# Reordering the first loads and splitting the last output products of a four-layer cross-attention and expert kernel on Trainium2

## The reference

```python
x = x + L0_xattn(layernorm(x), ctx, ...)      # 16 heads of 16, 1601 context rows of 192, with biases
x = x + L0_ffn(layernorm(x), ...)             # 16 experts, top 4 by groups, and a shared expert
x = x + L1_xattn(...);  x = x + L1_ffn(...)   # 16 heads; 8 experts, top 2, gelu
x = x + L2_xattn(...);  x = x + L2_ffn(...)   # 8 heads of 32; 8 linear experts, top 2
x = x + L3_xattn(..., mask, ...); x = x + L3_ffn(...)   # 16 heads, masked keys; 16 gated experts, top 2

# one attention
q, k, v = xn @ Wq + bq, ctx @ Wk + bk, ctx @ Wv + bv      # split by heads
att = softmax(q @ k.T * scale)                            # over the 1601 context rows
out = (att @ v) @ Wo + bo                                 # heads joined again
```

## Time and profile before

| | |
|---|---|
| median of 3 runs | 3855.93 us (3853.42 to 3857.38) |
| the profiled execution | 3857.22 us, its span 3855.5 us |
| mean granted TensorE clock in it | 0.966 of full |
| PE, DVE, ACT, POOL busy | 94%, 66%, 50%, 17% of the span |

### The profile page before, as it was taken

One profiled execution on the slowest core, in us unless ns is written; L12 is line 12 of the kernel. 1 busy time (PEld: TensorE's weight loads), 2 busy tenths in 40 slices (PEclk: granted clock), 3 DMA queues, 4 the chain that ended last, 5 costly groups with the idle time before them and its releaser, 6 DMA issues. The chain is left out here.

```text
span 3855.5 us, 50411 instructions
## 1 busy us (share of the span) xinstructions
PE 3615.5 (94%) x17554; PEld 1563.8 (41%) x17555; DVE 2536.7 (66%) x5373; ACT 1931.5 (50%) x2358; POOL 645.9 (17%) x940
## 2 busy tenths in 40 slices
PE   5999999799999999987997899999799999998996
PEld 2333333365533333325665333333433333332564
DVE  5888888456678888844223655553478888884523
ACT  3677777521147777762332444444203777777111
POOL 3200001200041010014221301010313001001242
PEclk8999999899999999998999899999799999999998
DMA  6300000123000000025001400000140000001144
GB/s 129 54 19 16 17 18 6 50 75 77 24 30 15 18 14 19 9 65 202 31 30 50 114 20 16 18 18 5 58 94 31 18 18 15 18 10 49 53 121 133
DMA packets 132653, 171.33 MB, mean 44 GB/s; under 512 B 38379, under 2 KB 106589, under 8 KB 130257
## 3 DMA queue, kind: packets, MB, share of 16 engines
q1 hardware_dynamic: 119280, 142.27, 13.2%
q0 software_dynamic: 10144, 26.08, 2.7%
q10 hardware_dynamic: 3008, 0.15, 0.1%
HBM read 131.27 MB, written 40.84 MB: 45 GB/s over the span
## 5 line engine op out<-in xcount | busy, mean ns | idle before, releaser
L1524 DVE TENSOR_REDUCE mx<-ps 128x1 f32<-128x400 f32 (+1 forms) x3584 | 1818.4, 566 | 495.3 <-PE ps L2259 483.9
L1257 ACT ACTIVATE probs<-ps,zero_col 128x1024 f32<-128x1024 f32 (+1 forms) x1040 | 1111.1, 1111 | 585.0 <-PE ps L2295 584.6
L2259 PE MATMUL ps<-k_stack,q_stack 97*128 97x400 bf16 (+1 forms) x3584 | 1076.5, 339 | 50.1 <-DMA k_stack<-k_parts 27.8
L2295 PE MATMUL ps<-q_stack,k_stack 100*128 100x512 bf16 (+2 forms) x3328 | 1056.9, 381 | 6.4 <-ACT probs L1257 6.4
L2309 PE MATMUL ps<-probs,v 128*32 128x512 f32 (+2 forms) x5824 | 891.5, 607 | 0.2 <-ACT probs L1257 0.2
L2259 PEld LDWEIGHTS ps<-k_stack,q_stack 97*128 97x128 bf16 x3584 | 290.4, 97 | 1049.2 <-DVE mx L1524 624.8
L1257 ACT ACTIVATE probs<-ps,mask_col 128x1024 f32<-128x1024 f32 (+1 forms) x416 | 439.5, 1110 | 158.6 <-PE ps L2295 158.6
L2295 PEld LDWEIGHTS ps<-q_stack,k_stack 100*128 100x128 bf16 (+2 forms) x3328 | 323.3, 100 | 345.0 <-ACT probs L1257 65.8
L2309 PEld LDWEIGHTS ps<-probs,v 128*32 128x32 f32 (+2 forms) x5824 | 140.1, 111 | 264.3 <-issue 248.8
L1674 DVE SCALAR_TENSOR_TENSOR x_res<-ps,comb,x_res 128x256 f32<-128x256 f32 x336 | 148.1, 479 | 63.0 <-PE ps L2559 57.5
L1325 ACT ACTIVATE h_t_s<-ps 128x512 f32<-128x512 f32 x80 | 47.8, 597 | 254.3 <-PE ps L2550 254.3
(11 more groups left out here) (293 smaller groups left out, 2715.0 us busy)
## 6 DMA issues: line engine op xcount, KB each, us to landing
q_stack<-q_parts SPq DMA_DIRECT2D x384, 64.0 KB, 2.2
q_parts<-qk_part SPq DMA_DIRECT2D x32, 384.0 KB, 2.5
w_up<-in_up SPq DMA_DIRECT2D x17, 704.0 KB
w_up_s<-in_expert SPq DMA_DIRECT2D x40, 256.0 KB, 2.7
k_stack<-k_parts SPq DMA_DIRECT2D x48, 200.1 KB, 7.1
k_stack<-k_parts POOLq DMA_DIRECT2D x48, 200.1 KB, 4.1
k_parts<-qk_part SPq DMA_DIRECT2D x24, 384.0 KB, 3.1
w_all<-in_up SPq DMA_DIRECT2D x8, 1024.0 KB, 12.6
```

What stands on the lines that cost most here:

```text
L1257: act.activation(PR[pair[0] % 4][0:r, :, :], PS[0:r, 2 * b:2 * b + 2, :], ACT.Exp, bias=mask_col[0:r, k:k + 1] if L == 3 else zero_col[0:r ...
L1524: ins = dve.reduce_max(MX4[g % 2][:, u, c:c + 1], PS[:, bank, 0:CK[c]], AX.X)
L2259: last = mm(PS[:, bank, 0:CK[c]], QS[g][0:97, slot_of(j), qt * P:(qt + 1) * P], KS[0:97, (g * hpg + j) * nsub, CKO[c]:CKO[c] + CK[c]], sta ...
L2295: last = mm(PS[0:r, b + i, :], KS[0:rows, (g * hpg + jj) * nsub + sub, k * P:k * P + r], QS[g][0:rows, slot_of(jj) + sub, :], start=sub == ...
```

## The change

First, the order of the loads at the start. Chunk 0 of x now comes behind the context tiles and key weights, before the query weights. The constant rows come before chunks 1 to 3. The value, output and their bias weights (`load_value_weights`) come behind the loads of group 0's keys. The nine loads of mask and gates go from ACT, before the fence, to SP, behind the queries of group 2. The six instructions that make the masks go from DVE to POOL, behind the split of key units 4 to 7. Query weights get a semaphore of their own (`s_wq`).

Second, in the prologue of layer 2 the `behind` list begins only after the first TPQ = 4 jobs.

Third, in the tail of each layer the four products of `o_t` index 0 get four banks of their own and stand ahead of, and behind, the turn of the reciprocals; the four of index 1 follow at the end, as a job "last".

```diff
             x_chunks = A["x"].rearrange("(c t p) d -> c p t d", t=TPQ, p=P)
-            sp.dma_start(X[:, 0:TPQ, :], x_chunks[0]).then_inc(s_x0, 16)
             sp.dma_start(C0[:], A["ctx_t"][0:P, :]).then_inc(s_ctx, 16)
             sp.dma_start(C1[0:DC - P, :], A["ctx_t"][P:DC, :]).then_inc(s_ctx, 16)
-            load_attention_weights(0)
+            load_key_weights(0)
+            sp.dma_start(X[:, 0:TPQ, :], x_chunks[0]).then_inc(s_x0, 16)
+            load_query_weights(0)
             fence(sp, fences)
+            load_constant_rows(0)
             for c in range(1, NQ):
                 sp.dma_start(X[:, c * TPQ:(c + 1) * TPQ, :], x_chunks[c]).then_inc(s_in, 16)
-            load_constant_rows(0)
...
             load_keys(sp, 0, 0)
+            load_value_weights(0)
             load_queries(0, (0, 1), 1)
...
             load_queries(0, (0, 2), 2)
+            sp.dma_start(mask_u8[:, 0:NK - 1], A["mask"][:, 0:P * (NK - 1)].rearrange("a (k p) -> p (a k)", p=P),
+                         allow_slow_non_contiguous=True).then_inc(s_mask, 16)
...
+            for L in range(4):
+                E = FFN[L]["E"]
+                sp.dma_start(GW[:, L], A[f"gw{L}"].rearrange("(k p) e -> p k e", p=P),
+                             allow_slow_non_contiguous=True).then_inc(s_gl, 16)
...
                         for u in range(4, 8):
                             split_keys(u, staged.take("key")[0])
+                        masks()
...
+                    elif job[0] == "last":
+                        t = (it - 1) * TPQ + 2 * job[1]
+                        x = X[:, t:t + 2, :]
+                        dve.tensor_tensor(x, x, PS[:, 2 * job[1]:2 * job[1] + 2, 0:D], ALU.add).then_inc(s_sf, 1)
...
             def first_query(m):
-                pe.wait_ge(s_wa, wa.at())
+                pe.wait_ge(s_wq, wq.at())
...
+                    elif job[0] == "last":
+                        for i in range(2 * job[1], 2 * job[1] + 2):
+                            last = mm(PS[:, i, 0:D], OT[:, 1, i * P:(i + 1) * P], WO[:, 1, :], start=False, stop=True)
...
                 every = len(jobs) // max(len(behind), 1)
+                lead = TPQ if L == 2 else 0
                 for n, job in enumerate(jobs):
                     side(job)
-                    if n % every == every - 1 and behind:
+                    if n >= lead and n % every == every - 1 and behind:
...
                 weigh(NG - 1, NK - 1)
                 njob[0] = 0
-                for job in [("den", NG - 1), ("spread", NG - 1)] + [("out", i) for i in range(TPQ // 2)]:
-                    side(job)
+                side(("den", NG - 1))
+                pe.wait_ge(s_ot, ot.at() + NG // 2 if ot.n > 0 else NG // 2)
+                for i in range(TPQ):
+                    mm(PS[:, i, 0:D], OT[:, 0, i * P:(i + 1) * P], WO[:, 0, :], start=True, stop=False)
+                    if i == 0:
+                        side(("spread", NG - 1))
+                for i in range(TPQ // 2):
+                    side(("last", i))
                 fence(pe, fences)
```

More of the change, by code:

```diff
@@ L346, in build @@
         s_wa = sem("s_wa")
+        s_wq = sem("s_wq")
         s_stat = sem("s_stat")
@@ L482, in _, with load_key_weights @@
             yd = [Count(q) for q in s_yd]
[L484 to L488, removed]
+            def load_key_weights(L):
                 wpad.step()
@@ L504, in load_attention_weights @@
                     sp.dma_start(dst, src, allow_slow_non_contiguous=True).then_inc(s_wa, 16)
+            def load_attention_weights(L):
+                load_key_weights(L)
+                load_query_weights(L)
+                load_value_weights(L)
             def load_constant_rows(L):
@@ L854, in link, with masks @@
                 pool.wait_ge(s_const, n[0])
+            def masks():
+                pool.wait_ge(s_mask, 3 * 16)
+                link(pool.memset(mask_col[:], 0.0))
+                for r, lo, hi in ((P, 0, NK - 1), (KREM, NK - 1, NK)):
+                    link(pool.tensor_copy(mask_col[0:r, lo:hi], mask_u8[0:r, lo:hi]))
+                    link(pool.tensor_scalar(mask_col[0:r, lo:hi], mask_col[0:r, lo:hi], 1.0, -MASKED,
+                                            ALU.subtract, ALU.mult))
+                link(pool.tensor_scalar(mask_row, mask_row_u8[:], 1.0, -MASKED, ALU.subtract, ALU.mult))
             def clear_attention_weights(L):
@@ L971, in _ @@
                 if L < 3:
-                    wa.step(16 * 7)
+                    wa.step(16 * 5)
                     pool.wait_ge(s_wa, wa.at())
@@ L1099, in _ @@
             rs = Count(s_rs)
[L1100 to L1110 removed]
+            wq = Count(s_wq)
             fence(act, fences)
@@ L1165, in scale_bias @@
             def scale_bias(scale):
+                wq.step(32 if wq.n < 96 else 16)
+                act.wait_ge(s_wq, wq.at())
                 act.activation(BQS[:], BQ[:], ACT.Copy, scale=scale).then_inc(s_bq, 1)
@@ L1421, in link @@
                 dve.wait_ge(s_v, v.at())
-            def masks():
-                dve.wait_ge(s_mask, 3 * 16)
-                link(dve.memset(mask_col[:], 0.0))
-                for r, lo, hi in ((P, 0, NK - 1), (KREM, NK - 1, NK)):
-                    link(dve.tensor_copy(mask_col[0:r, lo:hi], mask_u8[0:r, lo:hi]))
-                    link(dve.tensor_scalar(mask_col[0:r, lo:hi], mask_col[0:r, lo:hi], 1.0, -MASKED,
-                                           ALU.subtract, ALU.mult))
-                link(dve.tensor_scalar(mask_row, mask_row_u8[:], 1.0, -MASKED, ALU.subtract, ALU.mult))
             def variances(lo, hi):
@@ L1598, in _ @@
                     if L == 0:
-                        masks()
                         for u in range(4):
@@ L1639, in _ @@
                 njob[0] = 0
-                sides([("den", NG - 1), ("spread", NG - 1)] + [("out", i) for i in range(TPQ // 2)], NQ)
+                sides([("den", NG - 1), ("spread", NG - 1)] + [("last", i) for i in range(TPQ // 2)], NQ)
                 dve.wait_ge(s_sf, sf.at())
@@ L2178, in project_next @@
                     wk.step(16 * (3 if L < 3 else 2))
-                    wa.step(16 * (7 if L < 3 else 4))
+                    wq.step(16 * (2 if L < 3 else 1))
+                    wa.step(16 * (5 if L < 3 else 3))
                     pe.wait_ge(s_wk, wk.at())
@@ L2240, in side @@
                         pe.wait_ge(s_rw, rw.at())
-                    elif job[0] == "out" and job[1] == 0:
+                    elif job[0] in ("out", "last") and job[1] == 0:
                         ot.step(NG)
@@ L2350, in _ @@
                     wk.step(16 * 3)
-                    wa.step(16 * 7)
+                    wq.step(16 * 2)
+                    wa.step(16 * 5)
                     pe.wait_ge(s_wk, wk.at())
```

29 lines of the change are left out of this document (15 added, 14 removed).

## The result

The changed kernel takes 3842.5 us (median of 8 runs, 3839.1 to 3845.0) against 3856.4 us of the kernel before beside it (8 runs, 3849.6 to 3859.9): ratio 0.9959, 95% interval 0.995 to 0.9968, so 16 us faster by the ratio. The forecast was 3850, range 3838 to 3862.

The account below looks back on a forecast made before the run. PE, busy 94% of the span, was taken to bound the chunks, so gains come only where it waits or runs at lower clock. Tails -11.5, layer 2 prologue -2, start +7.5 sum to -6 us: 3850 us, range 3838 to 3862.

Parts of the forecast that it names:

- A: Rival: nine loads issue in 4 us, first turn hardly late, start -1, sum -14.5, 3841 us; chance 0.20.
- C: Rival: tails gain only 8.2 us because the clock falls at the first gap; sum -2.7, 3853 us; chance 0.12.
- Tails, -11.5: Four layer tails: four products fewer behind `o_t`, gaining 8.2 to 15.4 us by clock; the middle taken.
- Lead in layer 2, -2: Layer 2's prologue: four maxima jobs move into PE's 2.96 us stall; between 0 and -3 us.
- the 1 us that I named: Sign of a right forecast: layer 2's stall at the first turn under 1 us.
- Start, +7.5: Layer 0's start: maxima 6 us earlier, first turn 3.0 us later, 4.5 us of lost clock; bounds -3 to +13.
- the store of unit 0: Layer 0's start: key unit 0's store issued between 19 and 24 us, needing 3.3 us to land.
- value weights: Layer 0's start: their bytes in the queue delay group 2's queries, up to 4.0 us, 3 taken.
- nine loads: Layer 0's start: on SP they delay the stores of key units 4 to 7 and the first turn by 6 us.
- lost clock: Layer 0, behind the first turn: PE waits about 9 us more, then runs at 1.2 GHz, losing 4.5 us.
- Masks on POOL, 1 to 4 us: Layer 0's start: mask row on POOL ahead of the query split takes 1 to 4 us; costs 0, at most +2.
- B: Rival: small packets clog SP's queue, first turn 11 us later still, start +18.5, sum +5, 3861 us; chance 0.13.

Follow-up runs that it names:

- thrown away: Kernel before with four more products in each tail's gaps, results discarded, the old eight still behind `o_t`: 3847.2 us, ratio 0.9973.
- the start alone: Kernel before with only the new order of the first loads and the masks on POOL: 3862.1 us, ratio 1.0009.
- the tails alone: Kernel before with only the change of the tails: 3844.2 us, ratio 0.9959.
- the lead alone: Kernel before with only the later begin of the `behind` list in layer 2's prologue: 3854.0 us, ratio 0.9987.
- keys first: Changed kernel, SP's stores of key units 4 to 7 ahead of later query and key loads, nine loads and POOL's masks later: 3838.8 us, ratio 0.9949.
- the last kernels: Changed kernel with mask and gate loads moved to about 40 us, alone, with keys first, and with both but masks later: 3842.7, 3833.9, 3832.7 us.
- the nine loads later: Changed kernel with SP's nine loads behind its stores of key units 4 to 7, POOL's masks behind query chunk 1's splits: 3838.7 us, ratio 0.9942.

## Why the prediction was right, and where it was off

The direction was right, and the time lay inside the range, 7.5 us under the forecast. The size was not: 14 us by the medians, 16 by the ratio, against a forecast of 6. The range of 24 us also held the times of A and C and no change at all, so that the time lay in it says little; the steps say more.

*Tails, -11.5.* Right in mechanism, and the size was its far bound: 2.78 us per tail was 2.75 in the forecast for full clock, in all four layers. I took the middle because the clock might fall at the first gap. It did not, in any of the 36 tails of the nine traces with this part, and "thrown away" shows that it is the products in the gaps that hold it. The old tails of layers 1 and 2 were 6.16 and 6.49, not the 6.6 I took for all: -14.7 in place of -15.4, plus 0.5 from the gap phase itself, which ran at full clock too.

*Lead in layer 2, -2.* The mis-sized step. I counted the four jobs that move into the stall and gave the clock nothing, with -3 as the bound; it was -5.8, outside. The jobs gave 2.9. The rest is the clock, and not at the wait, behind which it is at 0.50 in both kernels, but where the prologue ends: I had counted five bare jobs there and not read the clock beside them. (The wait itself is 1.06 us, just over the 1 us that I named.)

*Start, +7.5.* The steps up to the turn came out: fence at 7.4 us; maxima 4.75 us earlier (forecast 6); value weights 2.3 us (forecast 3, by the queries of group 2 at 63.49); nine loads in 5.5 us on SP (forecast 6); turn at 77.9; clock at 0.50 behind it; lost clock 3.3 to 3.4 us (forecast 4.5). That the turn came exactly as forecast is luck: the maxima were 1.25 us less early and the two delays 1.25 us shorter. So it was with the store of unit 0 too: it was issued at 17.59, ahead of my 19 to 24, and landed at 24.62, after 7.0 us in place of my 3.3. In the trace it was +6.3. But the kernel with the start alone is only 3.5 us slower. Part of the difference is that the profiled execution of before had a lucky start. The first turn (L2324, L2331), in three executions of the old order: the kernel before,

```profile
74.92 0.66 PE L2324 MATMUL ps<-ident,probs 128*128 128x128 f32 x4 [1.35 <-ACT qk_part L1140]
```

the tails alone,

```profile
76.60 1.11 PE L2331 MATMUL ps<-ident,probs 128*128 128x128 f32 x4 [5.24 <-ACT qk_part L1140]
```

and the thrown-away products:

```profile
75.60 1.12 PE L2324 MATMUL ps<-ident,probs 128*128 128x128 f32 x4 [4.26 <-ACT qk_part L1140]
```

All three run the same code up to there. Where the clock came up late, PE was busy with slow maxima until just before the turn and kept its clock. The kernel before has 0.66 from 60 to 66 us:

```profile
60.00:66.00 6.00, 6.00 (x17) 3.18 (x16) 3.30 (x7) 0.92 (x3) 2.91 (x3) 0.66 0.87 139
```

Where it came up early, PE finished early, waited, and lost it. The tails alone:

```profile
60.00:66.00 6.00, 6.00 (x25) 3.48 (x24) 5.24 (x11) 1.11 (x4) 2.92 (x3) 1.00 1.01 152
72.00:84.00 12.00, 6.90 (x18) 3.78 (x19) 3.45 (x7) 3.19 (x10) 3.75 (x6) 0.52 0.28 88
```

The first exponential of the old order came at 118.65 and 118.36 (the lead alone) in the one kind of execution, at 122.30 and 124.33 in the other; mean 120.9. The new order's, in three (124.98, 125.04, and 121.44 with the start alone), has a mean of 123.8. The difference of 2.9 us agrees with the 3.5 measured (0 to 6.9), though seven executions are few. By both the start is about +3, and my +7.5 was more than twice that.

*Masks on POOL, 1 to 4 us.* The row took 5.66 us, above the bound, and it cost nothing there; in "keys first", where it came latest, PE did not wait for it either.

*The rivals.* A forecast 3841 us by a start of -1. The time is A's, but its mechanism did not happen: the turn was late, and what brought the time down were tails and lead. Both A's and my start were read against one execution. B's long delay did not happen at its place: the DMA engines had only a share of 0.40 there. Where they are loaded, at 41 to 51 us in the last kernels, issues behind a mask load did take several us. By the Trainium skill ("DMA: Bandwidth & Descriptors", "Issuing engines are not separate DMA queues") spreading loads over engines saves only the sequencer's time, "which is usually small"; this case agrees on what was given up, and that small time was 5.5 us on the queue for which the path waited. C's tails, 4.56 us, were seen in none of these nine traces. Its fall of the clock at the first gap does exist: without a product there it came in two of four tails.

What stays open: 2.7 us lost between the tails of layers 0 and 1, in code that did not change. The start alone shows 0.6 of it, the tails alone none. Other unchanged stretches differ as much between executions of the same code: the end of the experts of layer 1, between two table loads, took 49.1 us in the kernel before (2094.38 to 2143.48) and 45.7 with the products thrown away.

## What to carry to other kernels

Price a wait of the matrix engine by the stretch behind it as well: waits of 3.6 us and more cost 1.2 to 4 us more in clock at the start. In the tails useful work put into idle gaps, even a few products, paid twice. Look also for stretches where the engine is paced by another and half idle: in layer 2 the clock fell there, and not at the wait that I had priced. When a reorder takes loads off one queue, list what is queued behind their new place, and follow the first engine that waits for it. And before a start is judged by one trace, look at several executions of it: here the same code differed by 6 us.

## What the runs showed of the hardware

- Four f32 products of 128x256 whose results nobody reads, placed in the two gaps of each tail (idle for 0.85 and 1.50 us before in layer 0), made this kernel 10 us faster.
- The mask row, 1x1601 uint8 to bf16 on one partition, took 5.66 us on POOL against 0.99 on DVE, 5.7 times as long; the Trainium skill ("GPSIMD Engine Reference", "Elementwise — side-by-side cycle accounting") has a ratio of 1.96 for an f32 addition of 2048 elements.
- DVE's operation on 128x4 of the earlier trace rows ended with POOL's long memset each time it began beside it: 0.02 us behind its end in the kernel before (begun at 11.12, 3.77 us), in the changed kernel (12.49, 0.68 us) and with the nine loads later (12.91, 0.26 us). In the start alone, begun 0.12 us before that end, it took 0.17 us. So it became short because it began later against the memset, which was not over as I had forecast.
- Issues of DMAs on SP behind the load of 128x12 single bytes took 3.5 to 6.7 us in four traces while the DMA engines were loaded (share 1.03 or more): the second mask load 4.72 and 6.69, the value weights' two issues 3.50 and 4.55. The second mask load took under 1 us where the engines were not loaded, and 0.75 and 0.71 in two of these four traces, loaded too; the value weights took 0.98 where no mask load stood ahead. The Trainium skill ("DMA: Bandwidth & Descriptors", "Rules for kernel authors") says that a non-contiguous last dimension becomes one descriptor per element. The trace agrees as far as sizes go: ACT's queue, with the masks and gates on it, moved 1546 packets and 0.01 MB in the first 12 us of the kernel before. That this is what makes the issues long is not shown.
